# Identity attention's keys turned by transposes, with the mean taken from VectorE's sums, and a row's output products split five, one and two

## The chip, the cores and the metric

The kernel runs on one NeuronCore of one Trainium2 chip. The metric is the device time of one execution in microseconds (us). Lower is better.

## What is computed

The reference is a small audio tower. A tokenizer cuts 64 recordings into 128 patches of 16 samples and gives each patch 256 features. Then comes an attention without weights (this is where the change lies), then two layers of local attention and a gated feed-forward. Of the attention without weights, in the reference's own words:

```python
def _L0_attn_ref(x):                       # x: layernorm of the tokenizer's output
    B, T, D = x.shape                      # 64, 128, 256
    H = 16
    hd = D // H                            # 16
    xh = x.reshape(B, T, H, hd)
    x_centered = xh - jnp.mean(xh, axis=1, keepdims=True)
    corr = jnp.einsum('bthd,bThd->bhtT', x_centered, x_centered)
    corr = jax.nn.softmax(corr, axis=-1)
    out = jnp.einsum('bhtT,bThd->bthd', corr, xh)
    return out.reshape(B, T, D)
```

Keys and queries are the same: the normalised row, less its mean over the 128 tokens. The row of all this is one recording (128 tokens by 256 features), and there are 64 of them.

## The kernel before

The five engines each run a program of their own, written out by hand, and meet through semaphores. `front` (L119) holds tokenizer and identity attention of all 64 rows; `layers` holds the rest and starts while the last rows of the front are still under way.

**The front is a pipeline over steps.** `run_eights` (L98) calls each engine's `body` once per step t, and every stage has a lag: step t computes the hidden layer for a later group, the output of row t-8 (OUT), the statistics of row t-9 (STAT), the keys of row t-10 (CENT), the scores of row t-11 (SCORE), the weighting of row t-12 (WEIGH), the turn back and the end of row t-13 (TURN, DONE), and the stores of row t-14 (STORE). Inside a step, each engine's order is the order of the code. A step is called a row below, since one row leaves the pipeline per step. Every fourth step (u % 4 == 3) TensorE also turns four rows of input (L557), and two steps earlier VectorE prepares them (L454 to L457).

**TensorE's step** is: scores of row t-11 (L525, 16 products of 32-partition keys), the turn back (L534, four transposes), the centred keys (L546, four products), in every fourth step the input's transposes (L557), the first part of the output products (`row_out`: one product L504, then three products L510 to L512 for each of eight blocks k), half a hidden layer (L493), the row maxima turned (L572, in the text "the maxima's product"), output blocks, the maxima subtracted from the scores (L583), the last output blocks, the other hidden half (L493) and the weighting (L599). The next step's scores follow.

**The keys.** `v1` holds the normalised row, each head padded from 16 to 32 columns with ones. TensorE multiplies each of its four blocks of 128 columns by a constant 128x128 matrix `centre` (1 - 1/128 on the diagonal, -1/128 elsewhere), which turns the block and takes away the mean at once:

```python
for j in range(4):
    last = pe.matmul(ps_turn[:, j], v1[:, slot, 4 * j:4 * j + 4]..., centre[:], start=True, stop=True)
last.then_inc(s["cT_ps"], 1)                                       # L546
act.activation(cT[:, (u - CENT) % 2], ps_turn, ACT.Copy)           # L356, one copy of 128x512
```

The scores (L525) are products of `cT` with itself, so `cT` of a step is needed by the next step's L525.

**The bank `ps_turn`.** One PSUM bank takes, in turn within a step, the keys (L546), the turned maxima (L572) and the weighting's output (L599). L572 therefore waits for ScalarE's copy of the keys (`cT_ready`) as well as for VectorE's two halves of the maxima (`max_done`, L426).

**ScalarE's step** is: copy of the output row (L343), the normalised output n2 (L349, waits for GpSimd's shift L321), the copy of the keys (L356), in every fourth step the copy of the input (L362), the copy of the turned maxima (L368), tanh (L335), two exponentials (L375), tanh, the copy of the weighted values (L384).

**VectorE's step** is: the second half's activation (L399), the two maxima reductions (L426), reciprocal and scaling of the attention output (L434, L437), statistics (L444, L448), the first half's activation (L399), the normalised row v1 (L465), statistics of the result (L472, L476). **GpSimd's step** is: cast and remainder of one hidden half (L278, L282), the residual sum (L293, waits for L437), variance and power (L300, L303), cast and remainder of the other half, variance, power, mean and shift of the result (L311 to L321), and in steps 14 to 25, 29 to 40 and 44 to 51 a piece of the first layer's weights (L785, L788).

## Time and profile before

| what | value |
|---|---|
| runs | 2687.47, 2690.91, 2691.41 us; median 2690.91 us |
| the profiled execution | 2688.39 us, span of its instructions 2686.6 us |
| busy over the span | PE 97%, weight loads 83%, DVE 71%, ACT 63%, POOL 53% |
| mean granted TensorE clock | 0.989 |
| the front (steps with scores) | some 40 to 540 us of the span; 55 rows of it from 55.3 to 487.0 us |
| the two layers | the rest, to 2686.6 us |

Times of trace rows are in us from the span's start. A timeline row has start, length, engine, line, operation, output<-inputs, shapes, count and, in brackets, idle time before it with what ended it. Rows of one line that follow each other are merged into one, so the distance from a row's start to the next row's start is the time that its engine gave to it.

### The profile page before, as it was taken

To read this page: it belongs to the slowest core of one execution; us is meant where nothing else is said; L and a number is where in the kernel's file an instruction comes from. 1 tells how busy PE (TensorE), PEld (TensorE's weight loads), DVE (VectorE), ACT (ScalarE), POOL (GpSimd) and SP (SyncE) were. 2 spreads that over 40 slices of the span, in tenths; PEclk is the share of its full clock that TensorE was granted. 3 is DMA by queue.
4 is the path that set the end of the run, shared out by engine and by line. 5 is a ranking of instruction groups with operands and counts; after the bars stand their busy time and mean duration, and the time that the engine had idled before them with its cause. 6 is when DMAs were issued, how large, how long until landed. Compare 5 with 4: busy or idle time off the path is not lost.

```text
span 2686.6 us, 71253 instructions
## 1 busy us (share of the span) xinstructions
PE 2597.5 (97%) x25088; PEld 2230.8 (83%) x25088; DVE 1918.4 (71%) x3779; ACT 1702.8 (63%) x4184; POOL 1424.5 (53%) x1512
## 2 busy tenths in 40 slices
PE   7999999889999999988999998999999998999998
PEld 5888888768888888877888887888888887888887
DVE  7777777668878788776555646887788777666664
ACT  4666666557777777774444435777777787444442
POOL 7888888477777776652000006777777664000000
PEclk9999999999999999999999999999999999999999
DMA  2111111111111111121111111111111111222221
GB/s 48 37 48 36 44 36 38 40 43 43 51 38 50 41 37 39 41 67 58 58 53 55 52 34 45 40 48 41 50 38 41 40 36 57 69 82 66 80 73 47
DMA packets 165615, 130.35 MB, mean 49 GB/s; under 512 B 23239, under 2 KB 163689, under 8 KB 165462
## 3 DMA queue, kind: packets, MB, share of 16 engines
q1 hardware_dynamic: 163157, 119.80, 14.5%
q0 software_dynamic: 2304, 8.47, 1.1%
q8 instruction: 100, 1.64, 0.3%
q14 instruction: 54, 0.43, 0.1%
HBM read 77.47 MB, written 50.33 MB: 48 GB/s over the span
## 4 chain that ended last, share of the span: by engine, by line
PE 48%; DVE 21%; ACT 20%; issue 7%; SPq 2%; DMA 1%; DVEq 1%; POOL 0%; ACTq 0%; POOLq 0%
ACT attn_E L1058 15%; PE const_banks L1335 6%; PE const_banks L1336 6%; PE const_banks L1337 6%; DVE attn_neg_top L1231 6%; DVE attn_ss L1224 5%; DVE attn_rot_b L1208 5%; ACT attn_sq L1095 5%; PE const_banks L1473 3%; PE const_banks L1472 3%; PE const_banks L1471 3%; PE const_banks L525 3%; PE const_banks L510 3%; PE const_banks L599 2%; PE const_banks L511 2%
## 5 line engine op out<-in xcount | busy, mean ns | idle before, releaser
L1058 ACT ACTIVATE attn_E<-const_banks,attn_nbias,attn_rn 128x128 f32<-128x128 f32 x1024 | 452.8, 461 | 146.2 <-DVE attn_nbias L1236 146.2
L995 POOL TENSOR_TENSOR attn_qk<-attn_rot_a,attn_rot_b 128x1024 f32<-128x1024 f32 x128 | 303.4, 2370 | 354.1 <-issue 288.6
L982 POOL TENSOR_TENSOR ffn_rstd<-ffn_var,const_neg_half 128x4 f32<-128x4 f32 x32 | 32.3, 1009 | 687.9 <-DVE ffn_var L1161 687.9
L1346 PE MATMUL const_banks<-weights_w_hi,attn_xT_hi 128*128 128x512 f32 x768 | 315.3, 411 | 5.4 <-ACT attn_sq L1095 4.3
L1347 PE MATMUL const_banks<-weights_w_lo,attn_xT_hi 128*128 128x512 f32 x768 | 304.3, 396 | 0.0
L1348 PE MATMUL const_banks<-weights_w_hi,attn_xT_lo 128*128 128x512 f32 x768 | 304.0, 396 | 0.0
L1261 DVE SCALAR_TENSOR_TENSOR ffn_gated<-const_banks,weights_b_col,ffn_gate 128x512 f32<-128x512 f32 (+1 forms) x192 | 143.7, 748 | 216.6 <-ACT ffn_gate L1129 209.7
L1335 PE MATMUL const_banks<-ffn_xT_hi,ffn_w_hi 128*128 128x512 f32 x704 | 283.6, 403 | 6.9 <-DVE ffn_xT_lo L1173 5.4
L1336 PE MATMUL const_banks<-ffn_xT_lo,ffn_w_hi 128*128 128x512 f32 x704 | 280.0, 398 | 0.0
L1337 PE MATMUL const_banks<-ffn_xT_hi,ffn_w_lo 128*128 128x512 f32 x704 | 279.3, 397 | 0.0
L1129 ACT ACTIVATE ffn_gate<-const_banks,weights_b_col 128x512 f32<-128x512 f32 x160 | 110.1, 688 | 228.2 <-PE const_banks L1337 222.7
L1224 DVE TENSOR_REDUCE attn_ss<-attn_sq 128x16 f32<-128x1024 f32 x128 | 156.2, 1220 | 119.6 <-ACT attn_sq L1095 119.6
L1001 POOL TENSOR_TENSOR attn_rn<-attn_ssm,const_neg_half 128x8 f32<-128x8 f32 x128 | 210.9, 1648 | 31.3 <-DVE attn_ssm L1226 29.0
L1058 ACT ACTIVATION_READ_ACCUMULATOR attn_E<-const_banks,attn_nbias,attn_rn 128x1 f32 x1024 | 213.4, 208 | 0.0
L1008 POOL TENSOR_TENSOR attn_rn<-attn_ssm,const_neg_half 128x8 f32<-128x8 f32 x128 | 209.4, 1636 | 0.0
L1201 DVE TENSOR_TENSOR attn_rot_a<-const_banks,weights_cos_s 128x1024 f32<-128x1024 f32 x128 | 156.7, 1225 | 59.2 <-PE const_banks L1348 59.2
L1095 ACT ACTIVATE attn_sq<-const_banks 128x1024 f32<-128x1024 f32 x128 | 131.1, 1025 | 107.0 <-DVE attn_rot_b L1208 107.0
L1139 ACT ACTIVATE ffn_h_hi<-ffn_gated 128x512 fp32r<-128x512 f32 x160 | 101.3, 633 | 140.9 <-DVE ffn_gated L1261 140.9
L1186 DVE TENSOR_TENSOR attn_E<-attn_E,attn_rsum 128x512 f32<-128x512 f32 x256 | 179.6, 702 | 8.8
L1471 PE MATMUL const_banks<-ffn_w_hi,ffn_h_hi 128*128 128x256 f32 x640 | 179.5, 280 | 6.1 <-DVE ffn_h_lo L1269 6.1
L1472 PE MATMUL const_banks<-ffn_w_lo,ffn_h_hi 128*128 128x256 f32 x640 | 179.7, 281 | 0.0
L1473 PE MATMUL const_banks<-ffn_w_hi,ffn_h_lo 128*128 128x256 f32 x640 | 179.5, 280 | 0.0
(179 smaller groups left out, 8009.3 us busy)
## 6 DMA issues: line engine op xcount, KB each, us to landing
attn_x_res<-xa SPq DMA_DIRECT2D x128, 128.0 KB, 4.9
xb<-attn_x_new SPq DMA_DIRECT2D x128, 128.0 KB, 1.7
ffn_x_<-xb SPq DMA_DIRECT2D x32, 512.0 KB
h<-ident_h SPq DMA_DIRECT2D x64, 128.0 KB, 1.7
xa<-ident_n SPq DMA_DIRECT2D x64, 128.0 KB, 1.7
attn_x_<-xa SPq DMA_DIRECT2D x128, 64.0 KB
xa<-ffn_x_new SPq DMA_DIRECT2D x16, 512.0 KB, 3.6
ffn_add<-h SPq DMA_DIRECT2D x16, 512.0 KB, 6.5
```

The costliest lines, as they stand in the source:

```text
L995: pool.tensor_tensor(qk[:, slot].rearrange("p a n -> p (a n)"), rot_a[:].rearrange("p a h d -> p (a h d)"), rot_b[:].rearrange("p a h d -> ...
L1058: last = act.activation(E[:, r, i], ps_s[:, r, i * P:(i + 1) * P], ACT.Exp, bias=nbias[:, r, i:i + 1], scale=rn[:, slot, h:h + 1], accum_o ...
L1095: act.activation(sq[:].rearrange("p h d -> p (h d)"), ps_qk[:].rearrange("p a n -> p (a n)"), ACT.Square).then_inc(s["squared"], 1)
L1224: dve.tensor_reduce(ss[:], sq[:], AX_X, ALU.add).then_inc(s["normed"], 1)
L1335: pe.matmul(dst, w.w1_hi[:, kk, at], yT_hi[:, slot, kk], start=(kk == 0), stop=False)
L1336: pe.matmul(dst, w.w1_hi[:, kk, at], yT_lo[:, slot, kk], start=False, stop=False)
L1337: last = pe.matmul(dst, w.w1_lo[:, kk, at], yT_hi[:, slot, kk], start=False, stop=(kk == KD - 1))
L1346: pe.matmul(out_, xT_hi[:, slot, k], w.w_hi[:, k, cols], start=(k == 0), stop=False)
L1347: pe.matmul(out_, xT_hi[:, slot, k], w.w_lo[:, k, cols], start=False, stop=False)
L1348: last = pe.matmul(out_, xT_lo[:, slot, k], w.w_hi[:, k, cols], start=False, stop=(k == KD - 1))
L1471: pe.matmul(dst, h_hi[:, slot, k, tok], w.w2_hi[:, k], start=(k == 0), stop=False)
L1472: pe.matmul(dst, h_hi[:, slot, k, tok], w.w2_lo[:, k], start=False, stop=False)
```

## The change

- TensorE no longer multiplies by `centre`: the four blocks of v1 are turned by `pe.transpose` against the identity. `centre` and its preparation on GpSimd go.
- VectorE sums each turned row over its 128 tokens, negated, into `nsum` (a new 128x4 reduction of the 128x512 bank). It stands between the two halves of the maxima.
- ScalarE writes `cT` as 128 x value + nsum, in four activations (one per block, since the bias is one column per block), in place of one copy. Keys are thus 128 times as large and scores 128 x 128 times; the exponential takes a scale of 1/128².
- In every fourth step ScalarE's copy of the input stands ahead of these four.
- `row_out`'s blocks are split 5, 1 and 2 around L572 and L583, in place of 4, 2 and 2.

```diff
-                if on(CENT):
-                    need(act, s["cT_ps"], b + 1)
-                    need(act, s["S_ps"], b - 1)
-                    act.activation(cT[:, (u - CENT) % 2], ps_turn, ACT.Copy).then_inc(s["cT_ready"], 1)
                 if on(0) and u % 4 == 3:
...
                     act.activation(xT[:, u // 4], turned_bank(t)[0:STACK], ACT.Copy).then_inc(xT_ready, 1)
+                if on(CENT):
+                    b = t - CENT
+                    need(act, s["summed"], b + 1)
+                    need(act, s["S_ps"], b - 1)
+                    for j in range(4):
+                        last = act.activation(cT[:, (u - CENT) % 2, j], ps_turn[:, j], ACT.Identity,
+                                              bias=nsum[:, (u - CENT) % 2, j:j + 1], scale=float(TOKENS))
+                    last.then_inc(s["cT_ready"], 1)
...
-                        act.activation(E[:, (u - SCORE) % 2, 2 * g:2 * g + 2], ps_S[:, 2 * g:2 * g + 2], ACT.Exp
-                                       ).then_inc(s["exp_done"], 1)
+                        act.activation(E[:, (u - SCORE) % 2, 2 * g:2 * g + 2], ps_S[:, 2 * g:2 * g + 2], ACT.Exp,
+                                       scale=1.0 / TOKENS ** 2).then_inc(s["exp_done"], 1)
...
+                for g in range(2):
+                    if on(SCORE):
...
                         dve.tensor_reduce(top[:, 2 * g:2 * g + 2, 0:4],
                                           ps_S[:, 2 * g:2 * g + 2].rearrange("p k (j t) -> p k j t", j=4), AX_X,
                                           ALU.max).then_inc(s["max_done"], 1)
+                    if on(CENT) and g == 0:
+                        b = t - CENT
+                        need(dve, s["cT_ps"], b + 1)
+                        need(dve, s["cT_ready"], b - 1)
+                        dve.tensor_reduce(nsum[:, (u - CENT) % 2], ps_turn, AX_X, ALU.add, negate=True
+                                          ).then_inc(s["summed"], 1)
...
                     for j in range(4):
-                        last = pe.matmul(ps_turn[:, j], v1[:, slot, 4 * j:4 * j + 4].rearrange("p h d -> p (h d)"),
-                                         centre[:], start=True, stop=True)
+                        last = pe.transpose(ps_turn[:, j], v1[:, slot, 4 * j:4 * j + 4].rearrange("p h d -> p (h d)"),
+                                            c["ident"][:])
...
                 if on(OUT):
-                    row_out(t, i, u, 0, 4)
+                    row_out(t, i, u, 0, 5)
...
                 if on(OUT):
-                    row_out(t, i, u, 4, 6)
+                    row_out(t, i, u, 5, 6)
```

**TensorE, around the maxima's product, before** (L493 is the hidden half, L572 the maxima's product, L510 to L512 one output block, L583 the subtraction of the maxima):

```order
L493 MATMUL const_banks<-tok_xT,tok_w_stack 128x512
L572 MATMUL const_banks<-const_ident_b,ident_top 128x128
L510 MATMUL const_banks<-tok_wo_tok_hi,tok_hid_hi 128x256
L511 MATMUL const_banks<-tok_wo_tok_lo,tok_hid_hi 128x256
L512 MATMUL const_banks<-tok_wo_tok_hi,tok_hid_lo 128x256
L510 MATMUL const_banks<-tok_wo_tok_hi,tok_hid_hi 128x256
L511 MATMUL const_banks<-tok_wo_tok_lo,tok_hid_hi 128x256
L512 MATMUL const_banks<-tok_wo_tok_hi,tok_hid_lo 128x256
L583 MATMUL const_banks<-ident_topT,ident_sel 128x128 x16
```

**The same place in the changed kernel** (its lines are L501, L580, L518 to L520 and L591):

```order
L501 MATMUL const_banks<-tok_xT,tok_w_stack 128x512
L580 MATMUL const_banks<-const_ident_b,ident_top 128x128
L518 MATMUL const_banks<-tok_wo_tok_hi,tok_hid_hi 128x256
L519 MATMUL const_banks<-tok_wo_tok_lo,tok_hid_hi 128x256
L520 MATMUL const_banks<-tok_wo_tok_hi,tok_hid_lo 128x256
L591 MATMUL const_banks<-ident_topT,ident_sel 128x128 x16
```

One block of three products has moved from between the two to ahead of the hidden half.

**VectorE, a step of the changed kernel** (L400 is the activation that was L399, L427 a half of the maxima, L435 the new sums, L442 and L445 the old L434 and L437):

```order
L400 SCALAR_TENSOR_TENSOR tok_hid<-tok_th,const_banks 128x512
L427 TENSOR_REDUCE ident_top<-const_banks 128x2x4
L435 TENSOR_REDUCE ident_nsum<-const_banks 128x4
L427 TENSOR_REDUCE ident_top<-const_banks 128x2x4
L442 RECIPROCAL ident_rsum<-const_banks 128x16
L445 TENSOR_TENSOR ident_att<-const_banks,ident_rsum 128x256
```

The sums stand between the two halves, which followed each other directly before.

## Rows read from the trace of the kernel before

**Rows 1.** Stage table of 100 us of the front: length, busy per engine, clock, DMA.

```profile
100.00:200.00 100.00, 99.90 (x1549) 87.25 (x1546) 75.91 (x174) 68.39 (x119) 87.74 (x162) 1.00 0.15 45
```

**Rows 2.** The scores' line from 55 to 487 us: count, durations in ns, first and last start.

```profile
L525 PE MATMUL const_banks<-ident_cT x1764: 270/270/372, 55.3 to 487.0; 32*128 32x128 f32 x196
```

**Rows 3.** Timeline of TensorE, one ordinary row.

```profile
369.67 1.17 PE L525 MATMUL const_banks<-ident_cT 32*128 32x128 f32 x32
370.78 0.66 PE L534 MATMUL const_banks<-const_ident,ident_outT 128*128 128x128 f32 x4
371.27 1.06 PE L546 MATMUL const_banks<-ident_centre,ident_v 128*128 128x128 f32 x8
372.08 0.36 PE L504 MATMUL const_banks<-tok_w_stack,tok_xT 84*128 84x256 f32 x1
372.28 0.28 PE L510 MATMUL const_banks<-tok_wo_tok_hi,tok_hid_hi 128*128 128x256 f32 x1
...
372.63 0.28 PE L510 MATMUL const_banks<-tok_wo_tok_hi,tok_hid_hi 128*128 128x256 f32 x1
...
373.93 0.23 PE L572 MATMUL const_banks<-const_ident_b,ident_top 128*128 128x128 bf16 x1
...
374.85 0.40 PE L583 MATMUL const_banks<-ident_topT,ident_sel 32*128 32x128 bf16 x16
...
377.39 1.17 PE L525 MATMUL const_banks<-ident_cT 32*128 32x128 f32 x32
```

**Rows 4.** Timeline of ScalarE, the same row.

```profile
371.57 0.60 ACT L349 ACTIVATE ident_n<-ident_h,ident_shift,ident_rstd 128x256 f32<-128x256 f32 x1 [0.78 <-POOL ident_shift L321]
372.36 0.60 ACT L356 ACTIVATE ident_cT<-const_banks 128x512 f32<-128x512 f32 x1 [0.19 <-PE const_banks L546]
374.19 0.28 ACT L368 ACTIVATE ident_topT<-const_banks 128x128 bf16<-128x128 f32 x1 [1.23 <-PE const_banks L572]
374.37 0.60 ACT L335 ACTIVATE tok_th<-const_banks 128x512 f32<-128x512 f32 x1
375.31 1.94 ACT L375 ACTIVATE ident_E<-const_banks 128x1024 f32<-128x1024 f32 x2 [0.34 <-PE const_banks L583]
377.13 0.61 ACT L335 ACTIVATE tok_th<-const_banks 128x512 f32<-128x512 f32 x1
```

**Rows 5.** Timeline of VectorE, the same row.

```profile
370.90 2.36 DVE L426 TENSOR_REDUCE ident_top<-const_banks 128x8 bf16<-128x1024 f32 x2 [0.17 <-PE const_banks L525]
...
375.14 0.69 DVE L399 SCALAR_TENSOR_TENSOR tok_hid<-tok_th,const_banks 128x512 f32<-128x512 f32 x1
```

**Rows 6.** Groups by line, whole span: two activations with a column as bias and scale.

```profile
L1058 ACT ACTIVATE attn_E<-const_banks,attn_nbias,attn_rn 128x128 f32<-128x128 f32 x1024 | 452.8, 461 | 146.2 <-DVE attn_nbias L1236 146.2
L1041 ACT ACTIVATE ffn_xg<-const_banks,weights_b_col,weights_g_col 128x512 f32<-128x512 f32 x64 | 46.3, 774 | 8.5 <-PE const_banks L1319 8.5
```

**Rows 7.** Timeline of TensorE: scores of a row that turns input, and of the next.

```profile
353.79 1.17 PE L525 MATMUL const_banks<-ident_cT 32*128 32x128 f32 x32
...
361.93 0.84 PE L525 MATMUL const_banks<-ident_cT 32*128 32x128 f32 x20
```

**Rows 8.** Timeline of GpSimd, the row of rows 3.

```profile
373.96 0.74 POOL L293 TENSOR_TENSOR ident_h<-ident_att,tok_h 128x256 f32<-128x256 f32 x1 [0.51 <-DVE ident_att L437]
...
375.89 0.73 POOL L278 CAST tok_hid_hi<-tok_hid 128x512 fp32r<-128x512 f32 x1 [0.41 <-DVE tok_hid L399]
...
379.09 0.19 POOL L321 TENSOR_TENSOR ident_shift<-ident_zero,ident_prod 128x1 f32<-128x1 f32 x1
```

**Rows 9.** Timeline of GpSimd, a row with a piece of weights.

```profile
316.48 0.29 POOL L785 CAST weights_wo_hi<-weights_stage 128x128 fp32r<-128x128 f32 x1
...
317.25 0.61 POOL L278 CAST tok_hid_hi<-tok_hid 128x512 fp32r<-128x512 f32 x1
```

**Rows 10.** Timeline of TensorE in the last two rows with new keys.

```profile
520.54 0.23 PE L572 MATMUL const_banks<-const_ident_b,ident_top 128*128 128x128 bf16 x1 [0.99 <-DVE ident_top L426]
...
525.69 1.11 PE L534 MATMUL const_banks<-const_ident,ident_outT 128*128 128x128 f32 x4
526.60 1.91 PE L546 MATMUL const_banks<-ident_centre,ident_v 128*128 128x128 f32 x8
529.25 0.27 PE L572 MATMUL const_banks<-const_ident_b,ident_top 128*128 128x128 bf16 x1 [0.73 <-issue]
```

More of the change, by code:

```diff
@@ L145, in front @@
         v1 = n.sb("v1", [P, 4, IH, W])
-        centre = n.sb("centre", [P, P])
+        nsum = n.sb("nsum", [P, 2, 4])
         sel = n.sb("sel", [P, 4, P], BF16)
@@ L189, in front @@
         s = {k: n.sem(k) for k in (
-            "stat", "aggr", "eps", "rstd", "norm", "cT_ps", "cT_ready", "S_ps", "max_done", "mT_ps", "mT_ready",
+            "stat", "aggr", "eps", "rstd", "norm", "cT_ps", "summed", "cT_ready", "S_ps", "max_done", "mT_ps", "mT_ready",
             "shifted", "exp_done", "outT_ps", "outT_ready", "out_ps", "recip", "att_done", "h2_done", "stat2",
@@ L247, in front_pool @@
             pool.memset(zero[:], 0.0).then_inc(pads, 1)
-            for ap, value in ((centre[:], -1.0 / TOKENS), (sel[:], 0.0), (c["ident_b"][:], 0.0),
+            for ap, value in ((sel[:], 0.0), (c["ident_b"][:], 0.0),
                               (c["causal"][:], 0.0), (c["neg_half"][:], -0.5)):
                 pool.memset(ap, value).then_inc(cleared, 1)
-            pool.wait_ge(cleared, 6)
-            pool.affine_select(out=centre[:], in_=centre[:], compare_op=ALU.not_equal, fill=1.0 - 1.0 / TOKENS,
-                               base=0, pattern=[[-1, P]], channel_multiplier=1).then_inc(pads, 1)
+            pool.wait_ge(cleared, 5)
             for k in range(4):
@@ L269, in front_pool @@
             pool.wait_ge(wo_split, 2)
-            pool.wait_ge(pads, 5)
+            pool.wait_ge(pads, 4)
             def cast(t, i, u, half):
@@ L350, in body @@
                                    scale=rstd2[:, slot:slot + 1]).then_inc(s["n2_done"], 1)
-                if on(CENT):
-                    b = t - CENT
-                    need(act, s["cT_ps"], b + 1)
-                    need(act, s["S_ps"], b - 1)
-                    act.activation(cT[:, (u - CENT) % 2], ps_turn, ACT.Copy).then_inc(s["cT_ready"], 1)
                 if on(0) and u % 4 == 3:
@@ L414, in body @@
                     dve.tensor_tensor(wo_lo[:], wo_half[:], wo_hi[:].bitcast(F32), ALU.subtract).then_inc(wo_split, 1)
-                    dve.wait_ge(pads, 5)
+                    dve.wait_ge(pads, 4)
                 if isinstance(t, int) and t == 9:
@@ L419, in body @@
                     silu(t - 1, 1)
-                if on(SCORE):
-                    b = t - SCORE
-                    for g in range(2):
+                for g in range(2):
+                    if on(SCORE):
+                        b = t - SCORE
                         need(dve, s["S_ps"], b + 1)
@@ L540, in body @@
                     if isinstance(t, int) and b == 0:
-                        pe.wait_ge(pads, 5)
+                        pe.wait_ge(pads, 4)
                         pe.wait_ge(sel_made, 4)
```

## The prediction

> **What bounds the kernel now.** I read the table of stages first. In the front TensorE is busy all the time (99.90 of 100 us, granted clock 1.00), with GpSimd next at 87.74 [rows 1]. Then the scores' line: 32 records per row, so from 55.3 to 487.0 us 55 rows pass, 7.85 us each [rows 2]. The timeline shows no idle time of TensorE in a row: from one row's scores to the next is 377.39 - 369.67 = 7.72 us [rows 3], and 8.14 where input is turned [rows 7]. So whatever TensorE sheds comes off the row, until another chain is as long. The change touches nothing after about 540 us; there I expect no difference.
>
> Below, times in a row count from the start of its scores (369.67). The second chain is: scores, maxima (start 1.23, end 3.59) [rows 5], the maxima's product at 4.26 [rows 3], its copy 4.52 to 4.80 [rows 4], their subtraction at 5.18 [rows 3], the exponentials 5.64 to 7.58 [rows 4], the next scores at 7.72. It has slack in two places: 0.67 us ahead of the maxima's product, 0.38 ahead of the subtraction. At its end there is hardly any: the next scores wait for the exponentials, which end 0.14 before them. The split 5, 1, 2 uses the middle slack.
>
> **TensorE.** The eight records by `centre` take 372.08 - 371.27 = 0.81 us, four transposes of the same size 371.27 - 370.78 = 0.49 [rows 3]. The keys' transposes have the same shape, so I take 0.49: **0.32 us less per row**. The bounds are 0.81 (no saving, were they priced as products) and 0.49. The moved block is 372.63 - 372.28 = 0.35 us, and changes no sum. TensorE alone would then have the maxima's product at 4.26 - 0.32 + 0.35 = 4.29, the subtraction at 4.86 and the next scores at 7.40.
>
> **VectorE.** The second half of the maxima starts some 1.14 us after the first (2.36 for two of 1.22), so the sums can start at 2.37; their transposes end at 1.60 + 0.66 = 2.26, just ahead. A sum over 128x512 has no row. From below it is half of a half of the maxima, 0.61; from above a pass over 128x512 by another operation, 0.69 [rows 5]. I take 0.69, as a fixed part of the cost doesn't halve. The sums end at 3.06, the second half of the maxima ends at 2.37 + 0.61 + 1.22 = 4.20, its product can go 0.05 later: 4.25, ahead of 4.29. **VectorE costs nothing, by 0.04 us.** What it delays is dealt with at GpSimd.
>
> **ScalarE, the closest term.** Four activations of 128x128 from PSUM with one column as bias replace one copy of 0.60. A 128x128 copy takes 0.28, and the next starts 0.18 after it [rows 4]. Two columns (bias and scale) make 0.60 into 0.77 on 128x512 [rows 6 and 4], so one is worth 0.09: I take 0.37 each, starts 0.27 apart, 3 x 0.27 + 0.37 = 1.18 in all. Bounds: no cost for the column, 3 x 0.18 + 0.28 = 0.82; both columns' price, as in the 0.46 of 128x128 [rows 6], starts 0.35 apart, 1.51. They start at 3.10 (sums 3.06, and 0.04 to pass on) and end at 4.28; the maxima's product can go at 4.34, **0.05 late**. Then its copy ends 0.54 later, 4.88, the subtraction starts at 4.94, the exponentials 0.46 after it end at 7.34, the next scores start between 7.40 and 7.45. I take 7.45: 0.27 us less in an ordinary row.
>
> For four such activations the Trainium skill (ScalarE: Activation LUTs, What ACT_TABLE_LOAD costs) would give, as an estimate, 3 x 0.293 + 0.386 = 1.27 us: 186 ns plus 0.833 per element, 93 more for a column, 93 of overlap. By that the gain of an ordinary row would be 0.18 and the whole gain some 4 us smaller; this trace agrees on the column (0.09), but its own 128x128 copy is shorter than the page's base.
>
> **The queues behind.** The second half of the maxima ends 0.61 later, and so does what follows on VectorE. GpSimd's residual sum, which waited 0.51 at 373.96 (4.29), starts at 4.90. Its next cast stood 375.89 - 373.96 = 1.93 behind it, 0.41 of that waiting, so it can follow at 6.42; from that cast to the end of the shift it takes 379.28 - 375.89 = 3.39 [rows 8], so the shift is there at 9.8, which is 2.4 of the next row. ScalarE's n2 stands ahead of the four activations in its queue and ends at 3.06, just in time. VectorE's first activation waited for tanh in most rows and absorbs the delay. Not so in every fourth row, that with VectorE's preparation of input (the row of rows 3): there the activation at 375.14 (5.47) had no idle before it and moves to 6.08, the cast to 6.83, the shift to 2.8 of the next row, n2 to 3.45. The four activations of that next row come 0.3 late: maxima's product 4.64, and the row gains nothing. That is GpSimd's and n2's price.
>
> Rows that turn input: TensorE has 8.14 - 7.72 = 0.42 more ahead of the maxima's product, which it reaches at 4.71. ScalarE copies the input first, from 2.8 to 3.4, its four activations overlap it by 0.1 (as the two exponentials do: 1.94 for two) and end near 4.5. These rows gain 0.30.
>
> **Sum over the 55 rows:** 13 turning rows x 0.30 = 3.9; 14 rows behind a late n2, 0; 28 others x 0.27 = 7.6. In all 11.5. Weights' pieces stand in 32 rows and take GpSimd 317.25 - 316.48 = 0.77 us each [rows 9]; it has 0.5 to spare in a row. I take 0.15 us off in 10 of them: -1.5. At the end TensorE waits anyway, and the longer chain shows: the maxima's product at 520.54 waited for VectorE [rows 10] and moves by 0.7; in the row after it, where the products by `centre` take 1.9 us at half the speed, the sums and activations (0.69 + 1.18) replace a copy of 0.60, and four records of eight go: +0.5. That is +1.2, against 0.2 that four rows before it gain. Start of the pipeline: nothing. **Total: -11.5 + 1.5 + 1.0, some -9 us; I say -10**, as five rows before 55 us also gain a little. From the profiled 2688.4 this is 2678.4; the runs' median stands 2.5 above that execution, its lowest 0.9 below, so I forecast 2680 for a median.
>
> **The rivals.** About 0.2% (5.4 us) is what a measurement can tell from no change.
> - *TensorE's bound alone:* columns cost nothing and n2 is never late. 55 x 0.32 less 1 at the end: -17; from 2690 that is 2673. For it: every term on the other engines is within 0.1 us of hidden. Against it: the row behind the late n2. Chance 0.14, inside "faster".
> - *The copies are dear:* 1.51 us in all ends at 4.61, the maxima's product goes at 4.67, 0.38 late. Ordinary rows +0.06, turning rows -0.19, rows behind the late n2 +0.36: 28 x 0.06 - 13 x 0.19 + 14 x 0.36 = +4, and 1 at the end, 2693. With half the extra price it is 2686 to 2688; either way no change that can be told. For it: 128x128 with columns did take 0.46. Chance 0.11.
> - *Slower: the four don't overlap.* They start 0.46 apart, 1.84 in all, end at 4.94; the product goes at 5.00, 0.71 late, ordinary rows +0.39. With 0.69 behind a late n2 and 0.15 where input is turned: 28 x 0.39 + 14 x 0.69 + 13 x 0.15 = +22, 2711. It decides from 0.36 us between starts, where the row is 7.72 again. Against it: the copy of 0.28 is followed after 0.18 [rows 4], and nothing shows that a column takes the overlap away. Chance 0.06.
> - *The clock falls.* Transposes stand in every row already at a granted clock of 1.00 [rows 1 and 3]. At half the clock eight records take some 1.9 us for 1.06 [rows 10 and 3], and a row would be some 7 us longer, so two such rows undo the gain. The Trainium skill (TensorE: Matmul & The Clock Gate, Part 4) says that transpose mode doesn't count as busy in the same way as products; by that rule this is the danger. Chance 0.01.
> - *Sums not hidden:* the sums read late and hold the second half of the maxima. Each 0.1 beyond 0.69 costs 0.1 per row; from 0.9 the gain is under the limit. Chance 0.05, no change.
>
> **How the numbers follow.** Forecast as worked out (2675 to 2684) 0.58, with TensorE's bound 0.14 and small misses that still clear the limit 0.05: faster 0.77. Same: 0.11 + 0.05 = 0.16. Slower: 0.06 + 0.01 = 0.07. The range 2672 to 2690 goes from TensorE's bound to the middle of the dear copies and leaves out some 0.15.
>
> **What would show it.** Right: the keys' line with four records and 0.49 to the next; starts of the four activations 0.27 apart; the sums 0.69; rows of 7.4 to 7.45, one in four at 7.6 to 7.7, one at 7.8. Wrong: idle time of TensorE ahead of the maxima's product above 0.3 in ordinary rows, or rows after 540 us that differ.

## The result and the profile after

The changed kernel takes **2698.55 us** (median of 8 runs, 2696.91 to 2699.12), the kernel before 2691.01 (8 runs, 2687.47 to 2691.41): ratio 1.0031, 95% interval 1.0020 to 1.0042, **7.5 us slower**. The forecast was 2680.0, with a range of 2672 to 2690: the kernel was to get faster and got slower.

| what | before | after |
|---|---|---|
| profiled execution, its span | 2688.39, 2686.6 us | 2699.12, 2697.3 us |
| busy over the span: PE, weight loads, DVE, ACT, POOL | 97, 83, 71, 63, 53% | 96, 82, 73, 65, 53% |
| mean granted TensorE clock | 0.989 | 0.985 |

The stage table of the kernel after, for the stretch of [rows 1] (length, then busy per engine in the order PE, weight loads, VectorE, ScalarE, GpSimd; then granted clock and DMA):

```profile
100.00:200.00 100.00, 97.75 (x1499) 81.04 (x1498) 84.81 (x189) 75.74 (x156) 86.47 (x159) 1.00 0.14 44
```

TensorE was busy for 99.90 of these 100 us before; now it stands idle for 2.25 of them, at the same clock. VectorE has 8.9 more to do, ScalarE 7.4. The groups of the front's steady part, 55 to 487 us, show that each new operation costs what was forecast or less (busy us, mean ns of one | idle before):

```profile
L361 ACT ACTIVATE ident_cT<-const_banks,ident_nsum 128x128 f32<-128x128 f32 x220 | 62.6, 367 | 22.8 <-DVE ident_nsum L435 22.8
L435 DVE TENSOR_REDUCE ident_nsum<-const_banks 128x4 f32<-128x512 f32 x55 | 37.5, 681 | 0.0
L554 PE MATMUL const_banks<-const_ident,ident_v 128*128 128x128 f32 x220 | 33.0, 273 | 0.0
```

Then a whole row of TensorE, the one that follows the row in which VectorE prepares input, and the end of that one (L533 scores, L554 the keys' transposes, L512 and L518 to L520 output products, L501 a hidden half, L580 the maxima's product, L591 their subtraction, L607 the weighting):

```profile
378.86 0.28 PE L520 MATMUL const_banks<-tok_wo_tok_hi,tok_hid_lo 128*128 128x256 f32 x1
379.71 0.50 PE L501 MATMUL const_banks<-tok_xT,tok_w_stack 84*128 84x512 f32 x1 [0.57 <-DVE tok_hid L400]
380.15 1.08 PE L607 MATMUL const_banks<-ident_E,ident_v 128*32 128x128 f32 x32
381.16 1.17 PE L533 MATMUL const_banks<-ident_cT 32*128 32x128 f32 x32
382.26 0.66 PE L542 MATMUL const_banks<-const_ident,ident_outT 128*128 128x128 f32 x4
382.76 0.60 PE L554 MATMUL const_banks<-const_ident,ident_v 128*128 128x128 f32 x4
383.11 0.36 PE L512 MATMUL const_banks<-tok_w_stack,tok_xT 84*128 84x256 f32 x1
...
385.50 0.22 PE L580 MATMUL const_banks<-const_ident_b,ident_top 128*128 128x128 bf16 x1
...
386.08 0.40 PE L591 MATMUL const_banks<-ident_topT,ident_sel 32*128 32x128 bf16 x16
...
387.11 0.28 PE L520 MATMUL const_banks<-tok_wo_tok_hi,tok_hid_lo 128*128 128x256 f32 x1
387.38 0.49 PE L501 MATMUL const_banks<-tok_xT,tok_w_stack 84*128 84x512 f32 x1
387.81 1.08 PE L607 MATMUL const_banks<-ident_E,ident_v 128*32 128x128 f32 x32
388.82 1.17 PE L533 MATMUL const_banks<-ident_cT 32*128 32x128 f32 x32
```

The row takes 388.82 - 381.16 = 7.66 us. Up to the subtraction everything is where the prediction put it: four transposes instead of eight records, even 0.35 us to the next row for the forecast 0.49; the maxima's product at 4.34, the subtraction at 4.92. What isn't, is the end. **At the end of the prepared row the second hidden half (L501) starts at 379.71 only, after 0.57 us of idle time, and waits for VectorE's first activation, L400.** (The first activation is the one of the first hidden half; a prepared row is one in which VectorE prepares input.) VectorE in the same stretch:

```profile
377.31 0.42 DVE L445 TENSOR_TENSOR ident_att<-const_banks,ident_rsum 128x256 f32<-128x256 f32 x1
...
378.20 0.39 DVE L462 CAST tok_x_stack<-tok_x_tok 128x64 fp32r<-128x64 f32 x1
378.51 0.22 DVE L463 CAST tok_x_stack<-tok_x_tok 128x64 fp32r<-128x64 f32 x1
378.77 0.23 DVE L465 TENSOR_TENSOR tok_x_stack<-tok_x_tok,tok_x_stack 128x64 fp32r<-128x64 f32 x1
378.97 0.69 DVE L400 SCALAR_TENSOR_TENSOR tok_hid<-tok_th,const_banks 128x512 f32<-128x512 f32 x1
379.58 0.41 DVE L473 TENSOR_SCALAR ident_v<-tok_h,ident_mv,ident_rstd 128x256 f32<-128x256 f32 x1
...
386.64 0.69 DVE L400 SCALAR_TENSOR_TENSOR tok_hid<-tok_th,const_banks 128x512 f32<-128x512 f32 x1
387.60 0.68 DVE L473 TENSOR_SCALAR ident_v<-tok_h,ident_mv,ident_rstd 128x256 f32<-128x256 f32 x1 [0.27 <-POOL ident_rstd L301]
```

Both halves of the hidden layer are made in one PSUM bank. In `hidden`, TensorE waits with `need(pe, hid_done, b)` until VectorE has read the half before it, so L501's second product of a step waits for L400's first activation **of the same step**. In the prepared row VectorE has no idle time before L400 (378.97 follows 378.77), and of the 0.6 us of the sums 0.47 arrive there: it ends 6.76 into the row, for 6.29 in the kernel before (medians of the 13 prepared rows). L400 ends at 379.66, L501 follows 0.05 later. In the ordinary row the activation could still take up the delay, since it used to wait for ScalarE's tanh: it ends at 6.18 for 6.11 (medians again). But there TensorE is done with the output products earlier, at 6.07 for 6.33, so that it now meets the activation too: L400 ends at 387.33 and L501 follows at 387.38. The table of waits, 55 to 487 us, after (waiter <- what ended it: us in total, times, longest; PEld is TensorE's weight load):

```profile
POOL ident_h L291 <- DVE ident_att L445: 31.3, 54, 1.5
...
PEld const_banks L501 <- DVE tok_hid L400: 18.1, 49, 0.8
PEld const_banks L580 <- DVE ident_top L427: 12.8, 41, 0.5
...
PE const_banks L501 <- DVE tok_hid L400: 7.8, 14, 0.6
```

and the one line on the hidden half (L493) that the same table of the kernel before has:

```profile
PEld const_banks L493 <- DVE tok_hid L399: 0.2, 1, 0.2
```

In PE's line the wait comes 14 times (the 13 prepared rows and one other), in that of the weight loads 49 times. Ordinary rows take 7.57 to 7.67 (of eight rows, two take 7.77 and 7.83), the 13 prepared rows 8.25, rows that turn input 7.95: 55 rows take 434.1 us in place of 431.66.

The same by kind of row, for these two kernels and four of the experiments below (mean length in us; the last column is the length of the 55 rows):

| kernel | ordinary (29) | prepared (13) | turns input (13) | 55 rows |
|---|---|---|---|---|
| before | 7.74 | 7.78 | 8.15 | 431.7 |
| e7: transposes, plain copy, no sums, split 4, 2, 2 | 7.31 | 7.74 | 7.73 | 413.0 |
| e3: e7 with the split 5, 1, 2 | 7.51 | 7.79 | 7.94 | 422.1 |
| e2: e3 with the sums | 7.61 | 8.22 | 7.95 | 430.8 |
| after: e2 with four activations | 7.71 | 8.25 | 7.94 | 434.1 |
| e9: after with the weighting first | 7.73 | 7.70 | 8.04 | 428.7 |

The prepared rows lose 6.0 us in all, the ordinary ones gain 0.9 and the turning ones 2.7.

### The profile page after: what moved, and what is told of

Same layout as the page of the kernel before. It is cut to its first block, busy times and chain, and to the rows that moved or that the text cites. A ratio compares the mean times of both kernels' runs of the same rounds, so it can differ in the third digit from the quotient of the medians.

```text
span 2697.3 us, 71062 instructions
## 1 busy us (share of the span) xinstructions
PE 2594.3 (96%) x24832; PEld 2209.1 (82%) x24832; DVE 1969.8 (73%) x3843; ACT 1743.3 (65%) x4376; POOL 1417.2 (53%) x1510
## 3 DMA queue, kind: packets, MB, share of 16 engines
q1 hardware_dynamic: 163157, 119.80, 14.3%
## 4 chain that ended last, share of the span: by engine, by line
PE 43%; DVE 22%; ACT 20%; issue 9%; SPq 2%; POOL 2%; DMA 1%; DVEq 1%; ACTq 0%; POOLq 0%
ACT attn_E L1066 15%; PE const_banks L1343 6%; PE const_banks L1344 6%; PE const_banks L1345 6%; DVE attn_neg_top L1239 6%; DVE attn_ss L1232 5%; DVE attn_rot_b L1216 5%; ACT attn_sq L1103 5%; PE const_banks L1481 3%; PE const_banks L1480 3%; PE const_banks L1479 3%; PE const_banks L533 2%; PE const_banks L607 2%; SPq L931 2%; PE const_banks L518 2%
## 5 line engine op out<-in xcount | busy, mean ns | idle before, releaser
L427 DVE TENSOR_REDUCE ident_top<-const_banks 128x8 bf16<-128x1024 f32 x128 | 156.1, 1220 | 35.0 <-PE const_banks L533 35.0
```

## The experiments

Ratios are to the kernel before, measured on the same chip beside them (its medians there 2689.6 to 2690.8), with 95% intervals. Row times are from each kernel's profile.

**e1_prep_late.** VectorE's preparation of input behind its first activation:

```diff
+                if on(4):
+                    silu(t, 0)
                 if on(0) and u % 4 == 1:
...
-                if on(4):
-                    silu(t, 0)
```

> The changed kernel, with VectorE's preparation of input moved behind the first half's activation (L400), which it stood ahead of in one row of four. Theory Q (TensorE's second hidden half shares a PSUM bank with the first and waits for VectorE's activation of the first; the sums make that late): the rows that took 8.25 us take some 7.67, 13 x 0.58 = 7.5 us less than the changed kernel, 2691. Theory C (the four activations by ScalarE cost the time): no change, 2698. Theory N (ScalarE's n2, late by GpSimd's chain, holds the keys): a gain only if the row after gets shorter; it is already at 7.67, so at most 1 us.

Measured 2699.95, 1.0047 [1.0029, 1.0066]: the 2691 expected was missed. The prepared rows fell from 8.25 to 7.66, as expected from L501's wait, but the row behind each grew from 7.66 or 7.77 to 8.37 and more. There VectorE falls behind (its maxima start some 2 us into the row, for 1.24), and two of its operations take far longer than elsewhere. VectorE and GpSimd in this kernel:

```profile
284.81 0.64 DVE L467 TENSOR_TENSOR tok_x_stack<-tok_x_tok,tok_x_stack 128x64 fp32r<-128x64 f32 x1
285.38 1.50 DVE L473 TENSOR_SCALAR ident_v<-tok_h,ident_mv,ident_rstd 128x256 f32<-128x256 f32 x1
286.80 0.41 DVE L480 BATCH_NORM_STATS2 ident_stats<-ident_h 128x6 f32<-128x256 f32 x1
```

```profile
284.77 0.61 POOL L276 CAST tok_hid_hi<-tok_hid 128x512 fp32r<-128x512 f32 x1
285.46 1.27 POOL L280 TENSOR_TENSOR tok_hid_lo<-tok_hid,tok_hid_hi 128x512 fp32r<-128x512 f32 x1
```

L473 takes 0.41 where GpSimd's cast starts 0.15 behind it (379.58 above), 1.50 beside GpSimd's remainder, and ends 0.15 us after that (286.88 against 286.73). So the miss doesn't refute the wait at L501; moving the preparation turns it into another delay of the same size.

**e2_one_copy, e3_no_sums, e7_no_sums_split422** take the parts of the change away one after the other: the four activations become one plain copy again; then the sums go as well; then the split is 4, 2, 2 again. These three leave out the centring of the keys, and with it the scale of the exponential.

```diff
-                    for j in range(4):
-                        last = act.activation(cT[:, (u - CENT) % 2, j], ps_turn[:, j], ACT.Identity,
-                                              bias=nsum[:, (u - CENT) % 2, j:j + 1], scale=float(TOKENS))
-                    last.then_inc(s["cT_ready"], 1)
+                    act.activation(cT[:, (u - CENT) % 2], ps_turn, ACT.Copy).then_inc(s["cT_ready"], 1)
```

In e3 and e7 also (ScalarE's copy then waits for the transposes in place of the sums):

```diff
-                        dve.tensor_reduce(nsum[:, (u - CENT) % 2], ps_turn, AX_X, ALU.add, negate=True
-                                          ).then_inc(s["summed"], 1)
```

and in e7 also:

```diff
-                    row_out(t, i, u, 0, 5)
+                    row_out(t, i, u, 0, 4)
...
-                    row_out(t, i, u, 5, 6)
+                    row_out(t, i, u, 4, 6)
```

> The changed kernel with one plain copy of 128x512 in place of the four activations; the sums are still taken and waited for, but not used, so keys are not centred. Theory Q: VectorE's queue is as before, rows get at most 0.1 shorter (the maxima's product 4.25 for 4.34), 2694 to 2698. Theory C: the rows fall to TensorE's own 7.4, 55 x 0.25 = 14 less, 2685.

> As the run with one copy, and the sums are left out too: transposes, one plain copy, split 5, 1, 2; keys are not centred. Theory Q: VectorE is back to its old load, the second hidden half finds its bank free, rows are 7.4 us and 55 x 0.32 = 17 us go against the kernel before: 2674. If the transposes were no cheaper than the products: 2691.

> Transposes with one plain copy and no sums (keys not centred), with the old split 4, 2, 2. Theory S (the split 5, 1, 2 costs time by itself, since with the maxima's product it delays ScalarE's tanh and so the second hidden half): TensorE alone bounds the rows, 7.4 us and 7.8 where input is turned, 55 x 0.33 = 18 us less than before: 2673, some 8 less than the same kernel with 5, 1, 2. Rival: that kernel's rows of 7.5 have another cause (GpSimd); then 2681 again.

Measured 2695.39 (1.0019 [1.0009, 1.0029]), 2681.07 (0.9966 [0.9954, 0.9977]) and 2671.63 (0.9928 [0.9912, 0.9945]). e2 and e7 came as expected; e3 missed its 2674 by 7 us. From the kernel before upwards: transposes with a plain copy **-19.2**, the split 5, 1, 2 **+9.4**, VectorE's sums **+14.3**, four activations for one copy **+3.2**, together +7.7. The last step isn't clear of the noise, as its two intervals overlap, but the 55 rows of the profiles have it too (430.8 against 434.1 us). Of the 14.3 us of the sums 8.7 arise in the 55 rows, and most of the rest in the rows behind them, at the end of the front.

With the sums, e2's prepared rows are 8.20 to 8.26, as in the changed kernel, although its maxima's product stands 0.09 earlier (4.25); without them they are 7.79 on average (e3: 7.59 to 7.99). So the sums bring most of TensorE's idle time in the prepared rows (8.1 us in e2, 2.8 in e3), but not all of it. Even with neither sums nor four activations the cheaper transposes gain next to nothing there (e7: 7.74 for 7.78), where ordinary rows gain 0.43. The tables of waits of e3 and e7, 55 to 487 us, say why (L490 is the hidden half, L396 the activation):

```profile
PEld const_banks L490 <- DVE tok_hid L396: 12.9, 49, 0.7
PE const_banks L490 <- DVE tok_hid L396: 2.8, 8, 0.5
```

```profile
PEld const_banks L490 <- DVE tok_hid L396: 5.8, 13, 0.6
PE const_banks L490 <- DVE tok_hid L396: 2.6, 8, 0.4
```

In e7's prepared rows the activation ends at 6.31, as before, while TensorE is past its output products at 5.89 already. The slack at this link was 0.2 us or less in every kind of row, so anything that TensorE gains beyond that waits there.

**e5_before_split512, e4_split422.** The split by itself, on the kernel before and taken back in the changed one:

```diff
-                    row_out(t, i, u, 0, 4)
+                    row_out(t, i, u, 0, 5)
...
-                    row_out(t, i, u, 4, 6)
+                    row_out(t, i, u, 5, 6)
```

(e4 has it the other way round.)

> The kernel before with nothing but the split 5, 1, 2. The maxima's product comes 0.35 later, and with it ScalarE's copy and tanh, VectorE's activation (to end at 6.36) and so the second hidden half (6.41 for 6.31). Theory Q: rows 0.1 to 0.15 longer, +5 to +8, 2696 to 2699. Theories C and N: the order of the products costs nothing, 2691.

> The changed kernel with the old split 4, 2, 2. Here the sums and four activations set the maxima's product at 4.34 whatever the split. TensorE would reach it at 3.94 and wait 0.4, the subtraction starts at 5.27 for 4.93, the exponentials end at 7.67, ordinary rows 7.75 to 7.8 for 7.6 to 7.67; rows with input preparation stay at 8.25: +4, 2702. If the split were to blame in the changed kernel too: some 2691.

Measured 2703.0 (1.0049 [1.0032, 1.0066]) and 2702.64 (1.0046 [1.0029, 1.0063]). On the kernel before, the split costs 12 us, more than the 5 to 8 expected. It gives VectorE no work; it only brings the maxima's product late, 4.61 for 4.26, and with it ScalarE's tanh. The exponentials end where they did (7.61 for 7.58), but VectorE's activation ends at 6.46 for 6.11, TensorE would want the bank at 6.36, and the row takes 7.95 for 7.72. The line of the hidden half, 0.2 us in the kernel before, is here:

```profile
PEld const_banks L493 <- DVE tok_hid L399: 9.9, 48, 0.3
```

So the same link shows itself without sums, transposes or four activations. With the sums in, the product can't go before 4.33 anyway, and the split saves 4: the intervals of e4 and of the changed kernel overlap, but their 55 rows are 437.9 and 434.1 us. So it suits this change; it isn't what made it slow.

**e6_half_early.** TensorE makes the first hidden half directly behind the keys' transposes, and ScalarE its tanh ahead of the four activations (not in rows that turn input):

```diff
+                early = u % 4 != 3 and not (isinstance(t, int) and t < 12)
+                if on(4) and early:
+                    hidden(t, i, u, 0)
                 if on(OUT):
                     row_out(t, i, u, 0, 5)
-                if on(4):
+                if on(4) and not early:
                     hidden(t, i, u, 0)
```

> The changed kernel with the first hidden half directly behind the keys' transposes, and its tanh ahead of the four activations, in three rows of four. The activation by VectorE then waits for VectorE's queue alone. Theory Q: ordinary rows 0.05 to 0.1 shorter, rows with input preparation (VectorE's own queue) stay at 8.25: 2695. If the wait was for ScalarE's tanh only: those rows shorten too, 2688.

Measured 2694.72, 1.0014 [1.0004, 1.0024]. Ordinary rows 7.46 to 7.58, prepared rows still 8.17 to 8.25: in those, it isn't the tanh that L400 waits for, but VectorE's own queue.

**e8_early_actcasts.** e6, with the two casts of the prepared input on ScalarE and VectorE's subtraction of it ahead of the maxima:

```diff
-                    dve.tensor_copy(x_stack[:, slot, :, 0:PATCH], x_tok[:, slot]).then_inc(x_hi, 1)
-                    dve.tensor_copy(x_stack[:, slot, :, PATCH:2 * PATCH], x_tok[:, slot]).then_inc(x_hi, 1)
...
+                    act.activation(x_stack[:, slot, :, 0:PATCH], x_tok[:, slot], ACT.Copy).then_inc(x_hi, 1)
+                    act.activation(x_stack[:, slot, :, PATCH:2 * PATCH], x_tok[:, slot], ACT.Copy).then_inc(x_hi, 1)
```

> As the run before, and ScalarE makes the two casts of the input in its gap ahead of n2, while VectorE's subtraction goes ahead of the maxima, where VectorE waits for the scores: 0.7 us less in VectorE's queue between maxima and activation in one row of four. Theory Q: the rows of 8.25 fall to 7.55, 13 x 0.7 = 9 less: 2686, below the kernel before. If VectorE's queue is not the cause: 2695.

Measured 2688.92, 0.9994 [0.9984, 1.0004], for an expected 2686: no difference from the kernel before. Prepared rows 7.79 to 7.95, not 7.55: shorter, as 0.6 us of VectorE's queue are gone, but its subtraction now waits for ScalarE's casts and starts the maxima 0.2 to 0.3 late (1.47 to 1.52 for 1.24).

**e9_weigh_first, e11_before_weigh_first.** The direct test: no engine's work changes, TensorE only does the weighting first, so that it has 1.0 us of work while L400 ends. e11 is the same swap in the kernel before.

```diff
-                if on(4):
-                    hidden(t, i, u, 1)
                 if on(WEIGH):
...
+                if on(4):
+                    hidden(t, i, u, 1)
```

> The changed kernel with one edit on TensorE: the weighting (L607) ahead of the second hidden half (L501) in place of behind it. Everything stays in; no engine gets less work. Theory W (what the change lost is TensorE's wait at the second hidden half for VectorE's first activation, since both halves write one bank): the 1.0 us of the weighting now covers that wait. In the row with VectorE's preparation L501 comes at 7.0 for a bank that is free at 6.8, so these rows fall from 8.25 to 7.65; ordinary rows stay within 0.1 of 7.6, since the second tanh comes some 0.2 later and the turn back of the next row then waits for the weighted values' copy. 14 x 0.6 = 8 us less: 2691, between 2688 and 2694. Rival S (the prepared rows are long because VectorE's and GpSimd's chain as a whole is too long for them, so that n2 and v1 arrive late whatever TensorE does in between): rows stay at 8.2, or the next row takes over what they lose, 2697 to 2700.

> The kernel before with the same swap on TensorE (weighting ahead of the second hidden half) and nothing else, as a control. Theory W: there the second half's wait for VectorE's first activation is nothing (TensorE never stands idle in those rows), so the swap gains nothing, and the second tanh that comes 0.26 later makes the next row's turn back wait by up to 0.1: 2690 to 2697. Rival (the swap helps any version of this kernel, whatever the change did): 2680 to 2686.

Measured 2693.66 (1.0008 [0.9999, 1.0017]) and 2704.49 (1.0048 [1.0035, 1.0062]). e9 is inside its range, at the upper end; e11 is above its range of 2690 to 2697. The swap costs the kernel before 14 us, 0.27 in each row (7.99 for 7.72): half of it since the turn back waits for the weighted values' copy, so that the keys' products start 1.74 into the row for 1.60. In the changed kernel the same swap *gains* 5 us. Its prepared rows are 7.70 for 8.25, and the row behind is 7.70 to 7.75, so nothing is handed on; ordinary rows lose up to 0.13, rows that turn input 0.09. TensorE in a prepared row of e9, without idle time (here L605 is the weighting), and from its table of waits, in which L501 waits for L400 no more:

```profile
375.08 0.28 PE L520 MATMUL const_banks<-tok_wo_tok_hi,tok_hid_lo 128*128 128x256 f32 x1
375.29 1.08 PE L605 MATMUL const_banks<-ident_E,ident_v 128*32 128x128 f32 x32
376.30 0.51 PE L501 MATMUL const_banks<-tok_xT,tok_w_stack 84*128 84x512 f32 x1
```

```profile
PEld const_banks L542 <- ACT ident_outT L385: 14.6, 56, 0.3
PEld const_banks L533 <- issue: 13.9, 56, 0.2
PEld const_banks L501 <- issue: 11.1, 56, 0.2
PEld const_banks L580 <- DVE ident_top L427: 10.8, 42, 0.3
```

VectorE's L400 starts at 375.20 and ends at 375.89, 6.85 into the row, and the hidden half comes at 7.26. With the old order TensorE would have wanted the bank at some 6.2.

**e10_all_three.** e6, ScalarE's casts with VectorE's subtraction at its old place, and the swap.

> Everything of the changed kernel stays in. Edits: first hidden half and its tanh early (as in e6_half_early), the two casts of the prepared input on ScalarE behind the output row's copy (VectorE keeps the subtraction where it was, ahead of its first activation), and the weighting ahead of the second hidden half (as in e9_weigh_first). Theory W: no wait of TensorE for VectorE's first activation is left in any row, the prepared row is 7.5 to 7.6 like the others, rows that turn input 7.9. From 2694.7 of e6_half_early: 14 rows x 0.65 = 9 less, 2686, between 2682 and 2689, below the kernel before. Rival S: prepared rows of 7.9 to 8.2, 2690 to 2695. If the late second tanh costs more than the wait it replaces, ordinary rows are 7.7 and the time is 2690.

Measured 2692.57, 1.0007 [0.9998, 1.0016]. Prepared rows 7.70 like all ordinary ones: no wait for L400 is left, and the swap's own price (7.70 for 7.58) is in every row. The time is above the expected 2682 to 2689; it is the case that the expectation named last.

**e12_casts_on_act.** e10 without the swap, meant to beat both.

> A version meant to beat both. Everything of the changed kernel stays in. As e8_early_actcasts (first hidden half and its tanh early, the two casts of the prepared input on ScalarE), but VectorE's subtraction of the prepared input stays at its old place behind the statistics, so that it neither waits for ScalarE's casts nor holds up the maxima. Theory W: in the prepared row VectorE's first activation comes 0.6 earlier than in e6_half_early (two casts of 0.6 together are gone from ahead of it), at 5.5, and the second hidden half no longer waits beyond what it does in an ordinary row: 7.6 in place of 8.2 there (and of 7.8 to 7.96 in e8_early_actcasts). 14 x 0.3 = 4 us under e8_early_actcasts: 2685, between 2682 and 2688, faster than before by some 0.2%. Rival S (something else than this wait sets the prepared row or moves into the next one, as in e1_prep_late): 2689 to 2695.

Measured 2687.7, 0.9993 [0.9984, 1.0002]: 11 us under the changed kernel, and no measurable difference from the one before, where 0.2% less was expected. Prepared rows are 7.78 to 7.91, not 7.6. VectorE and TensorE there (L475 the subtraction, L412 the first activation, L511 the hidden half):

```profile
372.73 0.33 DVE L475 TENSOR_TENSOR tok_x_stack<-tok_x_tok,tok_x_stack 128x64 fp32r<-128x64 f32 x1
372.99 0.67 DVE L412 SCALAR_TENSOR_TENSOR tok_hid<-tok_th,const_banks 128x512 f32<-128x512 f32 x1
```

```profile
373.31 0.28 PE L530 MATMUL const_banks<-tok_wo_tok_hi,tok_hid_lo 128*128 128x256 f32 x1
373.71 0.50 PE L511 MATMUL const_banks<-tok_xT,tok_w_stack 84*128 84x512 f32 x1
```

Still the same wait, smaller: L412 ends at 373.66, L511 follows at 373.71. The row began at 367.36, so the activation ends at 6.30, and VectorE has had no idle time since the maxima began at 1.24; TensorE wanted the bank at 373.31 + 0.12, that is 6.07.

## Why the prediction was wrong

**The step that failed** is "**VectorE costs nothing, by 0.04 us**", and with it "whatever TensorE sheds comes off the row, until another chain is as long". In "The queues behind" I followed VectorE's first activation to GpSimd's cast, its shift and ScalarE's n2. I didn't ask what TensorE waits for from it, and so gave its second hidden half no term at all. Its own start I had right: absorbed in ordinary rows (5.49 for 5.42), and moved to 6.08 in the prepared row (measured 6.07). But one bank takes both halves, and comes free only with the end of the first activation of its own step. In the kernel before, that wait was 0.2 us in the whole front, so it had no row that pointed to it; the semaphore in `hidden` did.

The link failed from both sides. TensorE got to it earlier (6.07 for 6.33), and the activation got there later (6.76 for 6.29 in the prepared row). The prepared rows, forecast 0.27 shorter, are 0.47 longer: 6.0 us lost. The ordinary ones gain 0.9 us in all. e9 shows that the wait is the loss (covered with other work, prepared rows are 7.70 and the kernel gains 5 us, where the same swap costs the kernel before 14). e2 against e3 shows that the sums bring most of the delay in the prepared row, and e5 and e7 that the link holds without them.

Term by term, the rest:
- *TensorE.* Forecast 0.32 less per row. The transposes take 0.35, not 0.49, so it is 0.46, and e7's ordinary rows are 7.28 to 7.30 for 7.72: 0.43 less. The kernel gains 19 us there. The forecast was too small by 0.14: I had priced the keys' transposes by those of the turn back [rows 3], which still take 0.50 (382.26 to 382.76).
- *VectorE's sums.* Forecast 0.69 and the second half of the maxima at 4.20; measured 0.68 and 4.20. Right.
- *Four activations.* Forecast 0.37 each, 1.18 in all, product at 4.34, subtraction 4.94, exponentials until 7.34; measured 0.367, 1.14, 4.34, 4.92, 7.32. Right, and worth 3.2 us against the plain copy. Here the Trainium skill (ScalarE: Activation LUTs, What ACT_TABLE_LOAD costs), at 1.27 in all, was above the measurement.
- *Ordinary row.* Forecast 7.45 from the exponentials' end. Measured 7.66: L501 waits 0.15 past the last output product (387.11 + 0.12 = 387.23), and from it to the weighting are 0.43 us where the kernel before has 0.32 (its L493 at 375.99, L599 at 376.31); that its weights too are loaded late (the 49 waits above) is the likely reason, not shown by a run. Without the two TensorE would be at 7.40, and the exponentials would hold the row. The rows from 490.39 to 520.21, in which the hidden halves have run out, take 7.45 or 7.46, as forecast.
- *The row behind the prepared one, late n2.* Forecast: no gain, through GpSimd's late shift. It has 7.66, with n2 at 2.09, ahead of the activations' 3.10. The shift came when forecast, 10.21 us after the start of the prepared row (383.12 - 372.91; forecast 10.2). But that row had become 0.8 us longer than forecast, so the shift was there at 1.96 and not at 2.8 of the next. In e9, where the prepared row is 7.70, it comes at 2.6 and n2 ends at 3.33. So the mechanism is there; it puts off the activations by only some 0.05. (There are 13 such rows, not 14.)
- *The row that turns input.* Forecast 7.84, measured 7.95; there too the second hidden half waits for the activation, and has 0.42 us to the weighting (363.81 to 364.23) for 0.32. It is 7.94 in e3 as well and 7.73 in e7, so the split alone is enough to hold it, and the sums add nothing (e2: 7.95).
- *Weights' pieces, +1.5.* Not there: rows behind the last piece (from 365.25: 7.66, 8.25, 7.66, 7.95) are as long as those with one.
- *Start and end.* Forecast nothing and +1.0. The first rows' scores come 1.0 us later (56.29 for 55.29). The last steps with scores lose 1.6: 0.7 in the first without output products (7.45 for 6.78; TensorE is idle for 2.13 us ahead of its maxima's product) and 1.1 in the next (10.30 for 9.24, at half the clock in both), less 0.1 in those ahead of them; and 1.6 more up to the first square of the attention in layer 1 (555.56 for 548.91). In the stretch 500 to 560 the granted clock is 0.80, before 0.89: TensorE is at its lower level for some 24 us (527 to 551), before for some 14 (523 to 533 and 541 to 544). Whether that makes the second 1.6 wasn't tried, nor what makes the 1.0 at the start.
- *Sum.* Profile against profile: +1.0 at the start, +2.4 in 55 rows (forecast -11.5), +3.2 at the end of the front, +0.7 in layer 1, together +7.3, which is close to the +7.5 of the medians. The other 3.3 of the 10.7 between the two profiled executions arise in layer 2, where nothing differs; the profiled execution before stood 2.6 under its median.

**The rivals.** The slower side had two mechanisms, neither of which made the rows longer: activations that don't overlap (they do: four take 1.14), a falling clock in the front's rows (1.00 through the steady part, with eight transposes per row). By the rule of the Trainium skill on transposes (TensorE: Matmul & The Clock Gate, Part 4) that would have been the danger; no row of the steady front bears it out. At the end of the front it isn't settled: from 480 to 640 us the granted clock is 0.94 in the three kernels that multiply by `centre` (before, e5, e11), and 0.89 to 0.91 in all the others, which transpose, with or without the sums. TensorE also has more idle time there in some of them, and no run takes the two apart; e7 gains its 19 us even so, at 0.89. "Sums not hidden" asked only whether the sums hold the maxima, and had 0.05. The sign that I had named as the mark of an error, idle time ahead of the maxima's product above 0.3, didn't show either: the idle time stands at the other end of the row. The other sign, rows after 540 us that differ, did show, by the 1.6 us above.

**What stays open.** What the lower clock at the end of the front comes from and costs. And whether any placing of the sums beats the kernel before. e12 covers most of the wait and comes out level. Without the sums the gain is 19 us (e7), but then the keys aren't centred.

## What to carry to other kernels

When a queue is delayed by a new instruction, follow every semaphore that its later instructions raise, to every engine, with the time at which the receiver will want it, also where the wait is zero now. Do the same when an engine gets faster: it arrives earlier at every wait that costs it nothing today. Here both met at a link with 0.2 us of slack. Two halves of work in one PSUM bank make such a hidden link. And price an edit as a ladder (here -19, +9, +14, +3), since the parts of a change can be worth the opposite of what they are worth alone: the split costs 12 on the old kernel and saves 4 on the new one.

## What I had not expected of the hardware

- **VectorE and GpSimd stretch each other's operations from SBUF, and 0.1 us in their starts decides which.** The same 128x256 `TENSOR_SCALAR` takes 0.41 where it starts 0.15 ahead of GpSimd's cast; then the cast takes 0.73 in place of 0.61 (13 of the 55 rows after, 48 before). Where it starts 0.08 behind the cast it takes 0.68 (387.60 to 388.28), and in e1 1.50 beside GpSimd's remainder (285.38 to 286.88, GpSimd's until 286.73); there GpSimd's own are not longer (0.61 and 1.27). The order of work on VectorE thus has a price that no count of busy time shows, and e1 paid it. The Trainium skill (SBUF — State Buffer, Who interferes with whom) has an exclusive lock on a port pair that the two engines share. These rows agree in that one of the two keeps its length; but the stretched one ends 0.15 us behind GpSimd's, not its full 0.41.
- **A transpose of a 128x128 f32 block costs TensorE 0.09 us** (0.35 for four, then the next product; the turn back's four, behind the scores, take 0.50), where the product with a constant matrix takes two records and 0.20.
